# Cross attention 3: unscaled exponentials are turned, a second product with blocks of ones gives the sums, and VectorE scales the result

## The reference

```python
def _L1_xattn_ref(q, k, v, Wq, bq, Wk, bk, Wv, bv, Wo, bo):
    HEADS = 16; D_MODEL = 256; D_K = D_MODEL // HEADS
    qh = (q @ Wq + bq).reshape(B, LQ, HEADS, D_K).transpose(0, 2, 1, 3)
    kh = (k @ Wk + bk).reshape(B, LKV, HEADS, D_K).transpose(0, 2, 1, 3)
    vh = (v @ Wv + bv).reshape(B, LKV, HEADS, D_K).transpose(0, 2, 1, 3)
    scores = jnp.einsum('bhqd,bhkd->bhqk', qh, kh) * (1.0 / np.sqrt(D_K))
    attn = jax.nn.softmax(scores, axis=-1)
    out = jnp.einsum('bhqk,bhkd->bhqd', attn, vh)
    concat = out.transpose(0, 2, 1, 3).reshape(B, LQ, D_MODEL)
    return concat @ Wo + bo

x = x + jnp.tanh(g_xattn[1]) * _L1_xattn_ref(_layernorm(x), ctx_512, ctx_512, ...)
```

## Time and profile before

| | before |
|---|---|
| median of 3 runs | 1981.5 us (1980.46 to 1983.92) |
| the profiled execution's own time | 1976.22 us |
| its span | 1974.5 us |
| PE, DVE, ACT, POOL busy over the span | 91%, 65%, 52%, 35% |
| the stage of cross attention 3 | about 1673 to 1760 us of the span |

### The profile page before, as it was taken

How to read it: one execution, slowest core, us unless ns; L and a number is a source line. 1 busy time by engine, 2 the same in 40 slices (tenths; PEclk the granted TensorE clock), 3 DMA queues, 4 the chain that set the end, 5 groups by cost and what they waited for, 6 DMA issues and landing times. The chain is left out here.

```text
span 1974.5 us, 32334 instructions
## 1 busy us (share of the span) xinstructions
PE 1789.1 (91%) x11430; PEld 1164.3 (59%) x11430; DVE 1284.4 (65%) x2762; ACT 1035.4 (52%) x2194; POOL 693.3 (35%) x995
## 2 busy tenths in 40 slices
PE   6989999999899999998899989999999999872697
PEld 3445555555566666766567765557767555551597
DVE  5579999999734476232789963259999353868311
ACT  3489999999622354221677741147776211642232
POOL 0023333333334435142455641125555210450343
PEclk9999999999999998999999999999999999977799
DMA  3451111110000020020100002020000000037495
GB/s 122 136 165 45 44 45 44 44 44 2 1 1 1 0 60 1 1 65 8 39 6 5 4 7 70 0 59 3 7 7 7 6 0 12 6 114 186 117 329 157
DMA packets 102959, 97.23 MB, mean 49 GB/s; under 512 B 37056, under 2 KB 86544, under 8 KB 102672
## 3 DMA queue, kind: packets, MB, share of 16 engines
q1 hardware_dynamic: 99216, 90.84, 15.3%
q0 software_dynamic: 3584, 4.33, 1.1%
HBM read 78.23 MB, written 14.81 MB: 47 GB/s over the span
## 5 line engine op out<-in xcount | busy, mean ns | idle before, releaser
L613 DVE TENSOR_REDUCE negmax<-sps 128x1 f32<-128x1024 f32 x256 | 309.2, 1219 | 17.1 <-PE sps L535 12.6
L657 ACT ACTIVATE prob<-sps,negmax 128x1024 f32<-128x1024 f32 x256 | 285.7, 1117 | 23.2 <-DVE negmax L613 18.7
L1943 POOL TENSOR_TENSOR la_pr_x3kblk<-la_pr_x3kblk,la_ri 128x512 f32<-128x512 f32 x128 | 158.5, 1268 | 152.3 <-DVE la_ri L2042 152.3
L703 POOL TENSOR_TENSOR probT<-probT,after 128x128 f32<-128x128 f32 x256 | 116.9, 457 | 237.6 <-DVE probT L621 211.7
L2271 ACT ACTIVATE la_pr_x3kblk<-la_pr_x3kblk,la_nx 128x256 f32<-128x256 f32 x256 | 126.4, 495 | 100.9 <-DVE la_nx L2083 100.9
L535 PE MATMUL sps<-ks,qs 128*128 128x512 f16 x512 | 168.8, 381 | 7.8 <-PEq L42 3.1
L2493 PE MATMUL la_bs<-lf_zT,lfw 128*128 128x512 f32 x352 | 153.4, 594 | 0.0
L551 PE MATMUL tps<-ident,prob 128*128 128x128 f32 x704 | 125.3, 282 | 22.7 <-DVE probT L621 20.3
L551 PEld LDWEIGHTS tps<-ident,prob 128*128 128x128 f32 x704 | 79.7, 141 | 89.3 <-issue 43.7
L1953 POOL TENSOR_TENSOR la_qs<-la_qn,ores 128x256 f32<-128x256 f32 x128 | 97.1, 789 | 77.7 <-DVE la_qn L2099 77.7
L1585 PE MATMUL tx_s<-t_zT,tw 128*128 128x512 f32 x256 | 113.8, 593 | 1.1 <-ACT t_zT L1452 1.1
(11 more groups left out here) (378 smaller groups left out, 3870.4 us busy)
## 6 DMA issues: line engine op xcount, KB each, us to landing
w1e<-in_fc_T SPq DMA_DIRECT2D x16, 1024.0 KB, 5.7
w2e<-in_fc_T SPq DMA_DIRECT2D x16, 1024.0 KB, 8.8
qs<-q_parts SPq DMA_DIRECT2D x128, 64.0 KB, 1.9
ks<-k_parts SPq DMA_DIRECT2D x128, 64.0 KB, 1.9
q_parts<-parts SPq DMA_DIRECT2D x8, 512.0 KB, 3.7
k_parts<-parts SPq DMA_DIRECT2D x8, 512.0 KB, 3.6
tw<-in_L_xattn_a_li_w SPq DMA_DIRECT2D x4, 1024.0 KB, 8.2
lfw<-in_L_ffn_w SPq DMA_DIRECT2D x6, 640.0 KB
```

Of the source, the lines that this page charges most:

```text
L613: dve.tensor_reduce(negmax[:, n % 4:n % 4 + 1], slots[n % NS][:], X, ALU.max, negate=True).then_inc(s.max_done, 1)
L657: act.activation(prob[:, n % 3, :], slots[n % NS][:], ACT.Exp, bias=negmax[:, n % 4:n % 4 + 1], accum_out=rowsum[:, tile % 2, n % QUAD:n % ...
L703: pool.tensor_tensor(blk, blk, after[:], ALU.mult).then_inc(s.masked, 1)
L1943: ins = pool.tensor_tensor(prob[:, h:h + 2, :], prob[:, h:h + 2, :], rinv[:, h:h + 2].unsqueeze(2).to_broadcast([P, 2, 2 * P]), ALU.mult)
```

## The change

The exponentials are no longer scaled before they are turned: POOL's `share` is gone, and so are DVE's sums and 16 inverses per token (`shares`). PE turns a half as soon as the exponentials of the tile are there. After the 8 products with `vblk`, `weigh` makes 8 more with `mblk`, a block of ones with the same shape as a value block, into the second half of `ops`; under each output channel there then stands the sum of that channel's head. `outputs` moves from ACT to DVE: DVE takes the inverse of the 128 x 256 sums from PSUM into `inverse`, waits for it, and multiplies the 128 x 256 products by it into `res`. In DVE's order this stands behind `top` of a tile four ahead. POOL builds `mblk` once, in the stage before.

```diff
@@ cross_attention
-                total = sb(phase + "total", [P, 2, H], F32, c)
-                rinv = sb(phase + "rinv", [P, 2, H], F32, c)
+                inverse = sb(phase + "inverse", [P, MC * P], F32, c)
@@ gpsimd
-                        def share(t):
-                            pool.wait_ge(s.rinv_done, t + 1)
-                            for half in range(2):
-                                part = prob[:, t % NPB, half * 512:(half + 1) * 512].rearrange("p (h t) -> p h t", h=H // 2)
-                                pool.tensor_tensor(part, part, rinv[:, t % 2, half * H // 2:(half + 1) * H // 2].unsqueeze(2)
-                                                   .to_broadcast([P, H // 2, CT]), ALU.mult).then_inc(s.shared, 1)
@@ vector
-                        def shares(t):
-                            dve.wait_ge(s.exp_done, t + 1)
-                            dve.tensor_reduce(total[:, t % 2, :], heads(prob[:, t % NPB, :]), X, ALU.add).then_inc(s.totalled, 1)
-                            dve.wait_ge(s.totalled, t + 1)
-                            if t >= 2:
-                                dve.wait_ge(s.shared, 2 * (t - 2) + 2)
-                            dve.reciprocal(rinv[:, t % 2, :], total[:, t % 2, :]).then_inc(s.rinv_done, 1)
-
-                        for it in range(START, NT + 1):
-                            if live(it):
-                                shares(it)
+                        def outputs(t):
+                            dve.wait_ge(s.pv_done, t + 1)
+                            dve.reciprocal(inverse[:], ops[:, MC * P:2 * MC * P]).then_inc(s.inverted, 1)
+                            dve.wait_ge(s.inverted, t + 1)
+                            at = t % TPB * P
+                            dve.tensor_tensor(res[:, t // TPB * MC:(t // TPB + 1) * MC, at:at + P],
+                                              ops[:, 0:MC * P].rearrange("p (m t) -> p m t", m=MC),
+                                              inverse[:].rearrange("p (m t) -> p m t", m=MC), ALU.mult).then_inc(s.out_done, 1)
+
+                        for it in range(START, NT + 2):
                             if live(it + 2):
                                 top(it + 2)
+                            if live(it - 2):
+                                outputs(it - 2)
@@ scalar
-                        def outputs(t):
-                            act.wait_ge(s.pv_done, t + 1)
-                            at = t % TPB * P
-                            act.copy(res[:, t // TPB * MC:(t // TPB + 1) * MC, at:at + P],
-                                     ops[:, 0:MC * P].rearrange("p (m t) -> p m t", m=MC)).then_inc(s.out_done, 1)
...
-                            if live(it - 2):
-                                outputs(it - 2)
@@ tensor
                         def turn_probs(t, half):
-                            pe.wait_ge(s.shared, 2 * t + half + 1)
+                            pe.wait_ge(s.exp_done, t + 1)
...
                                                    pT[:, t % 2, spot(r) * P:(spot(r) + 1) * P], start=True, stop=True)
+                            for m in range(MC):
+                                for a in range(NC):
+                                    r = a * MC + m
+                                    mm = pe.matmul(ops[a * WIDE:(a + 1) * WIDE, (MC + m) * P:(MC + m + 1) * P],
+                                                   mblk[:].rearrange("p q d -> p (q d)"),
+                                                   pT[:, t % 2, spot(r) * P:(spot(r) + 1) * P], start=True, stop=True)
                             mm.then_inc(s.pv_done, 1)
@@ stage before, gpsimd, value_blocks
+                            pool.tensor_tensor(mblk3[:], vmask[:].unsqueeze(2).to_broadcast([P, 2, D3]),
+                                               vmask[:].unsqueeze(2).to_broadcast([P, 2, D3]), ALU.mult).then_inc(sc.v_built, 1)
```

## The result

The changed kernel takes 1990.21 us (median of 9 runs, 1985.10 to 1993.66) against 1981.5 for the kernel before (9 runs, 1976.64 to 1984.37): 8.7 us more. The ratio is 1.0044, with a 95% interval of [1.0029, 1.0058], so it is slower, by less than half a percent. Forecast were 13.8 us more, 1995.3, in a range of 1987 to 2010.

The account below looks back on a forecast made before the run. VectorE was taken to bound the stage's long part, but not its tail. Terms of -2.7, +10.7, +0.5 and +5.3 us gave 13.8 us more, 1981.5 + 13.8 = 1995.3 us, in a range of 1987 to 2010.

Parts of the forecast that it names:

- long part: The stage's rounds that VectorE sets, without gaps: 3.75 us a late round before, forecast 4.64 after the change.
- tail: The stage's end, not set by VectorE: 20.5 us instead of 15.2, 5.3 more, with TensorE's lower clock assumed throughout.
- rounds 0 and 1 without sums: Start of the stage: no sums and no outputs yet in these rounds, so round 2 starts 2.70 us earlier.
- 12 rounds, longer by: Rounds 2 to 13 on VectorE, each 0.89 us longer, +10.7 us.
- stalls: Two late rounds with a query projection, where VectorE waits for scores: 0.5 us in all.
- The inverse sets the round: VectorE's late rounds: inverse 1.93 us plus product replace sum and inverses, 4.64 us instead of 3.75.
- TensorE's round is 4.01 and covered: TensorE's round without projection: 8 more products add 0.39 us to 3.62, hidden behind VectorE's 4.64.
- The clock didn't fall in the long part: Judges a rival: TensorE's clock falls in these rounds; half of 12 hit gives 2006 us, all 2017; chance 0.14.
- streaming case: Rival: VectorE's inverse takes 0.42 us, TensorE decides with 4.01 us a round; 1981 to 1986 us; chance 0.11.
- faster case: Rival: TensorE absorbs the second product and the inverse costs under 1.0 us; 1977 us; chance 0.03.
- second rival: The inverse streams, VectorE's round is 3.2 us and TensorE's 4.01 decides; say 1985 us; chance 0.11.
- The stages behind shift as one: After the stage: the next stage's loads and the experts shift with it, so all 13.8 us reach the end.

Follow-up runs that it names:

- e1: Changed kernel with a copy from PSUM of the same 128 x 256 in place of the inverse; 1978.7 us, 0.9993 of the kernel before.
- e2: Changed kernel without the 8 products with ones, the inverse taken of the products with the values; 1986.9 us, 1.0038 of the kernel before.
- h4: Changed kernel with the inverse of only 128 of the 256 sums, used twice; 1980.7 us, 1.0003 of the kernel before.
- h3: Kernel before with 8 more TensorE products a tile, results not used; 1988.2 us, 1.0021 of the kernel before.
- e3: Changed kernel without the products with ones and with a copy of the value products in place of the inverse; 1975.2 us, 0.9983 of the kernel before.
- g4: Changed kernel with the products moved one round later, between the next tile's two turns; 1983.8 us, 1.0026 of the kernel before.
- h2: Changed kernel with turns of the unit matrix in TensorE's gaps of the last rounds; 1985.3 us, 1.0030 of the kernel before.
- g2: Kernel before with 8 turns of the unit matrix in TensorE's gaps in each of the last rounds; 1972.5 us, 0.9966 of the kernel before.

## Why the prediction was right, and where its sizes were off

The direction, the bound and the mechanism of the long part were right; the tail and one price were mis-sized, both to the high side, and the kernel is 8.7 us slower where 13.8 were forecast. The profile of the changed kernel allows the sum to be read part by part on the same marks (all from the start of the first maximum, in us):

| part | forecast | measured |
|---|---|---|
| rounds 0 and 1 without sums | -2.7 | -2.6 (1694.72 - 1682.08 = 12.64, against 15.19) |
| 12 rounds, longer by | 12 x 0.89 = 10.7 | 9.2 (1694.72 to 1751.88 = 57.16, against 46.80, less the stalls; 0.76 or 0.77 each) |
| stalls | 0.5 | 1.2 |
| tail | 5.3 | 1.0 (1751.88 to 1768.02 = 16.14, against 15.19) |
| sum | 13.8 | 8.8 |

The mark 1751.88 stands where VectorE's next instruction would have begun, 0.34 us behind the start of the last product of the long part.

**The inverse sets the round: right**, by e1, e2 and h4. **Its price was mis-sized**: I took 1933 ns, from a slope of 7.0 between 2 and 16; it is 1750 ns, by a slope of 6.25 above 16. That is 0.18 us a round, of which 0.06 came back elsewhere: the maximum takes 1.22 us here where it took 1.16 behind 16 inverses.

**TensorE's round is 4.01 and covered: right**, 4.06 measured in e1, and covered, since VectorE's round is 4.51 with the products and without them (e2). **The stalls by `project`** are where I had them, in the two late projection rounds (0.65 and 0.31 us) and also in an earlier one (0.23, at 1709.96); I had 0.5 in all. The two in VectorE's rows, where the idle time is given as 0.57 and 0.21:

```profile
1724.48 1.22 DVE L812 TENSOR_REDUCE x3nmax<-x3s 128x16 f32<-128x1024 f32 x1 [0.57 <-PE x3s L941]
...
1729.30 1.23 DVE L812 TENSOR_REDUCE x3nmax<-x3s 128x16 f32<-128x1024 f32 x1 [0.21 <-PE x3s L941]
```

**The tail was the part that I had wrong.** I wrote that I assumed the lower clock for all of it. In the first profile the clock was low only around one tile's products (1.08 us at 1752.11) and back at the next (0.64 at 1757.19). The first round took 5.08 us from product to product, near my 5.35, and the two behind it 3.74 and 3.73:

```profile
1752.11 1.08 PE L922 MATMUL x3o_ps<-x3pT,x3vblk 128*32 128x128 f32 x16 [1.45 <-DVE ores L825]
...
1757.19 0.64 PE L922 MATMUL x3o_ps<-x3pT,x3vblk 128*32 128x128 f32 x16 [0.71 <-ACT x3pT L845]
...
1760.93 0.64 PE L922 MATMUL x3o_ps<-x3pT,x3vblk 128*32 128x128 f32 x16 [0.67 <-ACT x3pT L845]
```

That is most of the 4.4 us by which the tail was too high, of 5.0 us in the whole sum; the rest is the last product and the cheaper inverse. Why the clock comes back here and not in the kernel before stays open. The number of products doesn't decide it by itself: h3 has as many and falls to 0.50 and stays there to its end, e3 has few and keeps 1.00 to its end, and e2, with the same work on TensorE as e3, falls to 0.50 and stays there. Nor does the length of one wait: in the changed kernel the clock fell behind a wait of 1.45 us for VectorE's product, in the kernel before behind one of 0.99 us, and g4 kept 1.00 through a wait of 1.45. What h2 and g2 show is only that the clock stays up with filler work, and what that is worth.

**The level was hit by luck.** I added to the profiled run's time the 5.3 us by which the median lay above it. The profiled run of the changed kernel, 1985.1 us, happens to be the shortest of its nine, 5.1 below their median.

**The rivals.** The clock didn't fall in the long part (1.00 up to 1750 us). The terms of the streaming case add up to 5.0 us, not the 4.8 that I wrote, which changes nothing. The streaming inverse and the faster case need an inverse under 1 us; h4 and e1 show that even then the kernel only draws level with before, since TensorE's 4.06 takes over, as the second rival had it. **The stages behind shift as one: right** within 1 us, 214.5 us behind the stage before and 215.2 after.

## What to carry to other kernels

A sum that is spread over all the channels it belongs to is 16 times as many inverses, and on VectorE an inverse costs by the element, here 6.25 ns against 1.2 for an addition of 1024 and 1.7 for a product of 256: take inverses where the sums are fewest, and only then spread them. Before work is taken from an engine with gaps in its round (POOL's 2 us a tile here) and another is loaded for it, look at which engine has no gap: here VectorE, which lost 1.4 us a tile and gained 2.2. Read an edit in one stage from that stage too; whole runs of one kernel differed by some 8 us, for reasons that lay in part ahead of it. And look at the last rounds of a pipelined stage on their own: the kernel before had 4 us to gain there by another order or by filler work on TensorE, without touching what bounds the long part.

## What was not expected of the hardware

- The price of a reciprocal has two slopes: 155, 169 and 253 ns at 2, 4 and 16 elements a partition (7.0 ns an element), then 553, 953 and 1753 ns at 64, 128 and 256 (6.25). Three points on a line at the small end did not give the slope at the large one.
- Source in PSUM or in SBUF makes next to no difference to it: 1757 and 1753 ns at 256.
- The granted clock of TensorE over one and the same stretch of one and the same program was 1.00 in one run and 0.60 in another (1525 to 1530 us, 157 us ahead of the stage), and that of the tail of the stage differed between kernels with the same work on TensorE (0.50 in e2, 1.00 in e3).
